# Token lists scattered to DRAM during attention, and expert outputs added into the output by DMA, in a gated cross-attention and mixture-of-experts kernel

## The reference

```python
x = x + tanh(g_xattn) * xattn(layernorm(x), ctx, ctx, Wq, Wk, Wv, Wo, ...)   # 16 heads of width 16
xn = layernorm(x)
probs = softmax(xn @ Wg)                       # N x 8
top_w, top_i = top_k(probs, 2)
top_w = top_w / (sum(top_w) + 1e-8)
combine = sum(one_hot(top_i) * top_w)          # N x 8
y = einsum(square(relu(einsum(xn, W1))), W2)   # every expert; W1 is 8 x 256 x 512, W2 8 x 512 x 256
x = x + tanh(g_ffn) * einsum(combine, y)
```

## Time and profile before

| | us |
|---|---|
| median of 3 runs (lowest to highest) | 647.26 (646.38 to 647.65) |
| span of the profiled execution | 644.1 |
| PE busy | 539.6 (84%) |
| DVE busy | 425.8 (66%) |
| ACT busy | 341.1 (53%) |
| POOL busy | 324.7 (50%) |

### The profile page before, as it was taken

One profiled execution on the slowest core, in us unless ns is written; L12 is line 12 of the kernel. 1 busy time (PEld: TensorE's weight loads), 2 busy tenths in 40 slices (PEclk: granted clock), 3 DMA queues, 4 the chain that ended last, 5 costly groups with the idle time before them and its releaser, 6 DMA issues.

```text
span 644.1 us, 12791 instructions
## 1 busy us (share of the span) xinstructions
PE 539.6 (84%) x3948; PEld 505.0 (78%) x3948; DVE 425.8 (66%) x1132; ACT 341.1 (53%) x716; POOL 324.7 (50%) x423
## 2 busy tenths in 40 slices
PE   4689999999999999996016999999999999999500
PEld 3689999889988999985016899999999999999500
DVE  3657778887888888786997455544445445444287
ACT  3477867676777767662500455555555555555200
POOL 4756745574566546332931555555555555553200
PEclk9899999999999999997555899999999999999955
DMA  7010212112111211112700234333332222221299
GB/s 234 17 34 26 84 50 83 50 52 81 51 66 51 83 50 34 35 41 96 227 0 8 77 119 133 108 108 112 111 107 74 75 82 76 74 77 56 74 390 360
DMA packets 42335, 59.04 MB, mean 92 GB/s; under 512 B 5291, under 2 KB 31583, under 8 KB 42271
## 3 DMA queue, kind: packets, MB, share of 16 engines
q1 hardware_dynamic: 34448, 39.01, 18.1%
q0 software_dynamic: 6944, 18.62, 9.3%
q10 hardware_dynamic: 879, 0.58, 0.3%
HBM read 36.31 MB, written 21.89 MB: 90 GB/s over the span
## 4 chain that ended last, share of the span: by engine, by line
PE 67%; DVE 15%; issue 7%; POOL 4%; DMA 2%; ACT 2%; SPq 1%; DVEq 0%; POOLq 0%; ACTq 0%
PE pair L738 38%; PE pair L837 12%; PE pair L885 4%; DVE x_all L1274 4%; PE pair L921 4%; POOL y_scratch L585 3%; PE pair L929 2%; DVE chosen L982 2%; DVE onehot_row L1154 2%; PE pair L811 2%; PE pair L896 2%; POOL xg L575 2%; PE pair L906 1%; PE pair L803 1%; PE pair L845 1%
## 5 line engine op out<-in xcount | busy, mean ns | idle before, releaser
L585 POOL DMA_INDIRECT y_scratch<-y_sb,scatter_at x71 | 70.0, 986 | 95.5 <-ACT y_sb L701 92.8
L1247 DVE TENSOR_TENSOR hTlo<-pair,hThi 128x512 fp32r<-128x512 f32 x71 | 49.1, 691 | 78.1 <-ACT hThi L715 78.1
L575 POOL DMA_INDIRECT xg<-xn_scratch,gather_at x71 | 69.0, 972 | 44.6 <-DVE gather_at L1208 23.3
L837 PE MATMUL pair<-vals,probT 128*128 128x136 f32 x640 | 87.9, 284 | 2.0 <-ACT probT L609 1.8
L837 PEld LDWEIGHTS pair<-vals,probT 128*128 128x128 f32 x640 | 78.5, 190 | 3.3 <-ACT probT L609 3.1
L738 PE MATMUL pair<-w2hi,hThi 128*128 x284 | 80.6, 284 | 0.1
L738 PE MATMUL pair<-w2hi,hTlo 128*128 x284 | 79.9, 281 | 0.0
L738 PE MATMUL pair<-w2lo,hThi 128*128 x284 | 79.8, 281 | 0.0
L1261 DVE TENSOR_TENSOR hsq<-pair,hrelu 128x512 f32<-128x512 f32 x71 | 49.1, 691 | 44.4 <-ACT hrelu L728 44.3
L728 ACT ACTIVATE hrelu<-pair 128x512 f32<-128x512 f32 x71 | 42.6, 600 | 55.3 <-PE pair L738 55.3
L738 PE MATMUL pair<-w1hi,xgThi 128*128 x142 | 62.5, 440 | 0.0
(11 more groups left out here) (162 smaller groups left out, 1496.1 us busy)
## 6 DMA issues: line engine op xcount, KB each, us to landing
raw<-in_L_ffn_W SPq DMA_DIRECT2D x16, 512.0 KB, 4.2
xs<-in_x SPq DMA_DIRECT2D x16, 256.0 KB, 2.8
x_scratch<-xs SPq DMA_DIRECT2D x32, 128.0 KB, 1.7
xn_scratch<-xn SPq DMA_DIRECT2D x32, 128.0 KB, 1.8
x_all<-x_scratch SPq DMA_DIRECT2D x8, 512.0 KB, 3.9
w1hi<-y_scratch SPq DMA_DIRECT2D x4, 1024.0 KB, 8.9
w1lo<-y_scratch SPq DMA_DIRECT2D x4, 1024.0 KB, 14.4
out<-x_all SPq DMA_DIRECT2D x8, 512.0 KB, 8.7
```

The costliest lines, as they stand in the source:

```text
L575: pool.indirect_dma_start(xg[j % XG][:, :], None, xn2_dram[:, :], bass.IndirectOffsetOnAxis(ap=gather_at[:, j:j + 1], axis=0)).then_inc(d_ ...
L585: pool.indirect_dma_start(y_dram[:, :], bass.IndirectOffsetOnAxis(ap=scatter_at[:, j:j + 1], axis=0), y_sb[j % 2][:, :], None).then_inc(d_ ...
L837: mm = pe.matmul(v_bank[:, 0:UH * VW], probT[u % 2][:, i, :], vals[:, b, c, i, :], start=(i == 0), stop=(i == KC - 1))
L1247: dve.tensor_tensor(hTlo[j % 2][:, :, :].rearrange("p c n -> p (c n)"), bank[2 + j % 2][:, :], hThi[j % 2][:, :, :].rearrange("p c n -> p ...
```

## The change

**Routing on DVE** is done for seven groups of four tiles and two of two (`GROUPS`), with the steps of `route_steps`. `count` starts at N times the expert number, so that `placed` and `at` give at once the place of a choice in a list tensor in DRAM (`list_at`, an integer). The weights are now computed there as well (`part` to `weight1`, one exponential on ACT per group), for each tile and choice into `meta` beside the token number. PE counts with eight products for a group of four (four for one of two).

**The lists** are written by POOL during attention: for each tile and choice one indirect DMA scatters 128 pairs (token number, weight) of 8 bytes into `list_dram`, 64 DMAs in all, four in each of two neighbouring slots per group (`list_stores`). SP fills the list tensor at the start with 3 DMAs (token numbers 0 to 127, weight 0), and for the first block of each expert, by 16 PE products with a one-hot and one more DMA, a token that the expert does not get (`cand_step`). After attention DVE computes from the counts which block of the list is tile j's (`block_at`), POOL gathers 80 blocks of 1 KB by one indirect DMA into `lists`, PE transposes token numbers and weights, DVE copies `gather_at` and ACT copies `tile_w`.

**`w2lo`** is computed by DVE: four of its eight pieces before the copy of `gather_at`, four behind it. All eight pieces of W2 have a buffer of their own.

**The output**: x1 is stored straight to `out` during attention. In the expert stage ACT scales y with `tile_w` as it copies it, and POOL scatters it with `compute_op=ALU.add` into `out`, at the same `gather_at`. As two tiles can hold the same token, the scatter of tile j waits until that of tile j - 1 has landed (`d_acc`). The reload of x1, the loads of `y_dram`, the last additions and the stores of the output are gone; SP waits for the last scatter.

```diff
+        def list_stores(s):

+            for r, (t0, n) in enumerate(GROUPS):
+                first = 2 * (t0 + n - 1) + (14 if r else 17)
+                if first <= s < first + 2:
+                    h = n // 2
+                    return r, [t0 + (s - first) * h + i for i in range(h)]
 ...
+        route_steps = [["best0", "equal0", "lowest0", "key0", "pick0"],
+                       ["masked", "best1", "equal1", "lowest1", "part"],
+                       ["key1", "pick1", "both"],
+                       [None, None, "place", "count", "placed", "at"],
+                       ["sum", "tiny", "one", "inverse", "weight0", "weight1"]]
 @block.sync
...
-                    sp.dma_start(x1_rows[:, t, :], xs[t // GT % XBUF][:, t % GT, :]).then_inc(d_x1[t // GT % XBUF], 16)
+                    sp.dma_start(out_rows[:, t, :], xs[t // GT % XBUF][:, t % GT, :]).then_inc(d_x1[t // GT % XBUF], 16)
...
-            for i in range(2):
-                sp.wait_ge(d_ys[i], 16 * len(range(i, NJ, 2)))
-            for c in range(NT // CT):
-                sp.dma_start(y_in[c], y_rows[:, c * CT:(c + 1) * CT, :, :]).then_inc(d_yin[c], 16)
-            for c in range(NT // CT):
-                sp.wait_ge(v_out, c + 1)
-                sp.dma_start(out_rows[:, c * CT:(c + 1) * CT, :], x1_all[:, c * CT:(c + 1) * CT, :]).then_inc(d_out, 16)
+            sp.wait_ge(d_acc, 16 * NJ)
 @block.gpsimd
...
+                stores = list_stores(s)
+                if stores:
+                    r, tiles = stores
+                    pool.wait_ge(d_cand, 16)
+                    pool.wait_ge(v_meta, 1)
+                    pool.wait_ge(v_route, max(routed_at["at", r], routed_at["weight1", r]))
+                    for t in tiles:
+                        for k in range(CHOICES):
+                            pool.indirect_dma_start(
+                                list_dram[:, :], bass.IndirectOffsetOnAxis(ap=list_at[:, k, t:t + 1], axis=0),
+                                meta[:, t, k, :], None).then_inc(d_list, 16)
...
-            for k in range(E):
-                pool.wait_ge(a_w2hi, k + 1)
-                pool.tensor_tensor(part_of(w2lo, k), raw2[k % W2BUF][:, :], part_of(w2hi, k).bitcast(F32),
-                                   ALU.subtract).then_inc(p_w2lo, 1)
+            pool.wait_ge(d_list, 16 * CHOICES * NT)
+            pool.wait_ge(v_block, 1)
+            pool.indirect_dma_start(lists[0:NJB, :, :].rearrange("p k w -> p (k w)"), None, list_blocks[:, :],
+                                    bass.IndirectOffsetOnAxis(ap=block_at[0:NJB, 0:1], axis=0)).then_inc(d_block, 16)
...
                 pool.wait_ge(a_y, j + 1)
-                pool.wait_ge(v_lists, 1)
-                pool.indirect_dma_start(y_dram[:, :], bass.IndirectOffsetOnAxis(ap=scatter_at[:, j:j + 1], axis=0),
-                                        y_sb[j % 2][:, :], None).then_inc(d_ys[j % 2], 16)
+                if j:
+                    pool.wait_ge(d_acc, 16 * j)
+                pool.indirect_dma_start(out_flat, bass.IndirectOffsetOnAxis(ap=gather_at[:, j:j + 1], axis=0),
+                                        y_sb[j % 2][:, :], None, compute_op=ALU.add).then_inc(d_acc, 16)
 @block.scalar
...
                 if j >= 2:
-                    act.wait_ge(d_ys[j % 2], 16 * (j // 2))
-                act.activation(y_sb[j % 2][:, :], bank[6 + j % 2][:, 0:D], ACT.Copy).then_inc(a_y, 1)
+                    act.wait_ge(d_acc, 16 * (j - 1))
+                act.activation(y_sb[j % 2][:, :], bank[6 + j % 2][:, 0:D], ACT.Copy,
+                               scale=tile_w[:, j:j + 1]).then_inc(a_y, 1)
 @block.tensor
...
+                    dst = shared_place["count", r][:, 0:(n + 1) * E].rearrange("p (t e) -> p t e", e=E)
+                    pe.matmul(dst[:, 0:n, :], counters[:, 0, :], both[:, 0:n, :], start=True, stop=(n == 1))
+                    for i in range(n - 1):
+                        pe.matmul(dst[:, i + 1:n, :], counters[:, 1, :],
+                                  both[:, i:i + 1, :].broadcast_to([P, n - 1 - i, E]), start=False, stop=(i == n - 2))
+                    for i in range(n):
+                        mm = pe.matmul(dst[:, n, :], counters[:, 1, :], both[:, i, :], start=(i == 0), stop=(i == n - 1))
```

More of the change, by code:

```diff
@@ L250, in build @@
-        YW = CT * CHOICES * D
-        y_in = [w[:, i * YW:(i + 1) * YW].bitcast(F32).rearrange("p (t k d) -> p t k d", k=CHOICES, d=D)
-                for w in (w1hi, w1lo) for i in range(E * EW // YW)]
+        need_i = [place(ctx, f"need_i{i}", [P, E], I32) for i in range(2)]
+        need = place(ctx, "need", [P, E])
+        spare = place(ctx, "spare", [P, E])
+        sums = place(ctx, "sums", [P, E, E])
+        taken = place(ctx, "taken", [P, E])
+        ended = place(ctx, "ended", [P, E])
@@ new lines, in route_step @@
+                if kind == "at":
+                    with nc.allow_low_precision(reason="sums of one place below 2 ** 16 and of zeros"):
+                        return dve.tensor_reduce(list_at[:, :, ts], placed[:, :, 0:n, :], AX.X, ALU.add)
+                if kind == "part":
+                    return dve.tensor_tensor(share[:, 0:n, :], logits[:, ts, :], over_e(best[:, 0:n], E + 1), ALU.subtract)
+                if kind == "sum":
+                    dve.wait_ge(a_share, g + 1)
+                    return dve.tensor_reduce(total[:, 0:n], share[:, 0:n, 0:E], AX.X, ALU.add)
@@ new lines, in _ @@
+            link(dve.tensor_reduce(taken[:, :], sums[:, :, :], AX.X, ALU.add))
+            tt(ended[:, :], taken[:, :], C("level"), ALU.is_ge)
+            tt(skipped[:, :], ended[:, :], spare[:, :], ALU.mult)
+            link(dve.tensor_reduce(skip[:, :], skipped[:, :], AX.X, ALU.add))
+            dve.tensor_tensor(block_at[:, :], skip[:, :], C("tile"), ALU.add).then_inc(v_block, 1)
+            link(dve.tensor_reduce(expert[:, :], ended[:, :], AX.X, ALU.add))
+            dve.tensor_scalar(expert[:, :], expert[:, :], float(E - 1), float(EW), ALU.min, ALU.mult).then_inc(v_expert, 1)
@@ new lines, in _, with split_w2 @@
+            dve.wait_ge(t_expert, 1)
+            dve.tensor_copy(expert_at[:, :], bank[7][0:1, 0:P]).then_inc(v_places, 1)
+            def split_w2(k):
+                dve.wait_ge(a_w2hi, k + 1)
+                dve.tensor_tensor(part_of(w2lo, k), raw2[k][:, :], part_of(w2hi, k).bitcast(F32),
+                                  ALU.subtract).then_inc(v_w2lo, 1)
+            for k in range(E // 2):
+                split_w2(k)
+            dve.wait_ge(t_lists, 1)
+            dve.tensor_copy(gather_at[:, :], bank[6][:, 0:NJB]).then_inc(v_gather, 1)
@@ L1244, in _ @@
+            for k in range(E // 2, E):
+                split_w2(k)
             for j in range(-3, NJ):
```

447 lines of the change are left out of this document (191 added, 256 removed).

## The result

The changed kernel takes 725.92 us (median of 4 runs, 724.88 to 730.69); the kernel before took 647.19 us on the same chip. The ratio is 1.123, with a 95% interval of 1.1193 to 1.1267: slower by 79 us, where 627 us was forecast. The time lies above the forecast's range too (593 to 677).

A forecast was written before the change was run, and what follows sets the result against it. PE was taken to bound attention and the expert stage, a DVE chain the gap, memory traffic with DVE the end. 644.1 + 12 - 24.4 + 27.2 - 34.4 = 624.5 us of span, forecast 627 us, range 593 to 677.

The forecast's parts named there:

- The expert stage, forecast +27.2: Expert stage: serial adding scatters slow the pace from 3.49 to 3.8 us over 70 steps, adding 27.2 us.
- Rival 2: Expert stage: DRAM read and write come one after the other; slower overall from a 4.08 us pace, 677 us; chance 0.25.
- the ring: Expert stage loop: one scatter's start to landing, 3.5 us, plus 0.3 us until the next DMA starts; pace 3.8 us.
- The round trip: Expert stage: an adding scatter's start to landing, taken as 3.5 us; up to 3.2 us was held free.
- Attention, forecast +12: Attention: list scatters on POOL delay `xnTlo` and PE gets 48 more products; together taken as 12 us more.
- Upper bound +35: Attention: each list scatter takes 1.5 us, later norm scales stall ACT, and all of it reaches PE: 35 us more.
- rival 3: Attention: list scatters cost 35 us instead of 12, with the forecast's pace: 650 us; chance 0.08.
- Between the stages, forecast -24.4: Gap before the expert stage: after 16 list scatters and the gather, PE starts at 331.1 instead of 355.55, saving 24.4 us.
- The end, forecast -34.4: After the last scatter: loads, additions and stores go; 3.5 us of landing and 0.1 for SP remain, saving 34.4 us.

The follow-up runs named there:

- lists_spread: The changed kernel with one list scatter per attention slot instead of four in each of two slots, last two groups unchanged: 719.5 us, ratio 1.1094 to the kernel before.
- no_add: The changed kernel with a plain scatter in place of the adding one, all waits kept, output rows overwritten: 642.5 us, ratio 0.9937 to the kernel before.
- two_targets: The changed kernel with odd tiles added into a scratch tensor, each target with its own chain of waits, merge left out: 636.5 us, ratio 0.9843.
- no_cand: The changed kernel without the step that finds tokens outside each expert for the first blocks: 722.3 us, ratio 1.1136 to the kernel before.
- w1lo_slot1: The changed kernel with the w1 pieces one slot earlier in attention: 719.1 us, ratio 1.1087 to the kernel before.
- w2lo_last: The changed kernel with all eight `w2lo` pieces behind the copy of `gather_at`: 732.9 us, ratio 1.1306 to the kernel before.
- best1: dist2 with list scatters spread over the slots, no step for tokens outside each expert, and w1 pieces one slot earlier: 606.4 us, ratio 0.9367 to the kernel before.
- lists_late: The changed kernel with all 64 list scatters behind POOL's attention work: 769.1 us, ratio 1.1893 to the kernel before.
- dist2: The changed kernel with each adding scatter waiting for the last but one, and list padding naming tokens from the middle: 637.5 us, ratio 0.9834 to the kernel before.

## Why the prediction was wrong

**The expert stage, forecast +27.2, measured +87.1.** This step failed first. The mechanism was right: one DMA in flight, a wait in each tile, everything else at the scatters' pace. Rival 2 stated it and named its point: slower from a pace of 4.08 us. Two terms of the ring were too small. The round trip was taken as 3.5 us and is 3.81 on the mean: 70 x 0.31 = 22 us. The time from a landing to the next start was taken as 0.3 us and is 0.79: 70 x 0.49 = 34 us. The six long steps add 4. Together 60, the whole miss of 59.9. The second is the graver: it also lowers the round trip that is free, from 3.2 us to 3.49 - 0.79 = 2.7. The 0.3 us came from two DMA instructions that POOL had queued and could start one behind the other. That POOL slept before is not the difference. In the kernel before it had waited 23.30 us for DVE's `gather_at`, and its DMA instruction at 351.30 started 0.29 us behind the end of

```profile
350.81 0.20 DVE L1208 TENSOR_SCALAR gather_at<-code 128x71 int32<-128x71 f32 x1
```

In `lists_spread` it started 0.27 us behind the landing of a DMA of SP (125.62 + 14.8 = 140.42, then 140.69). The 0.77 to 0.79 us stand where POOL waited for the landing of an indirect DMA that it had issued itself. No row of the kernel before has that case, and why it takes longer is open. This term is also why the range failed: its upper end, 4.2 + 0.3 = 4.5 us a step, varied the round trip and kept the gap fixed. `no_add` and `two_targets` fix the blame: without the add 82 of the 87 us are gone (243.8 against 238.8 us from first to last scatter), without its being serial all of them (238.7).

By the rule cited of the Trainium skill (Collectives: The Full Stack), the add costs a second read and an estimated 0.3 us; the trace has 3.8 us against 2.4, so 1.4 us. It doesn't bear this rule out as a price for latency, though as one for throughput nothing here speaks against it (`two_targets`).

**Attention, forecast +12, measured +40.6.** The bunches of list scatters do delay `xnTlo`, as the prediction said, but by more: PE waited 3.0 to 3.2 us in three groups, and 4.33 in the one with `klo`, where 1.6 was worked out. The prediction took the phase of the kernel before and moved the queue in it; its forecast put nothing on the norm scale, 1.7 us late in its own working, which only the upper bound names. The norm scale holds ACT, that holds the exponential and the transpositions, and PE comes to the next wait late and slow (granted clock 0.94 against 0.99). Upper bound +35 was meant for this and was too low, since two further costs were missing. DVE's `outside` and `onehot` work was not counted at all, only its 16 PE products: 7 us by `no_cand`. And `placed` beside `w1lo`: the earlier trace rows has that very operation at 2.37 us beside POOL's `w2lo`, and the prediction noted it where it went, without asking where else it would stand beside a wide POOL operation: in most routing groups (the median of its nine instances is 2.04 us). Moving it off gave 7 us (`w1lo_slot1`). With the 23 us of the list scatters that makes 37 of the 39 us by which attention fell behind. The 81 us that rival 3 added to POOL count all 64 list scatters; 16 of them stand behind attention.

**Between the stages, forecast -24.4, measured -16.6.** The order was right: a row of list scatters on POOL, then the lists' gather. Missing: 4.4 us of the scatter of 5.32 us; 1.3 us, as the last scatter landed 3.66 us after its start, not 2.4; 0.8 us from that landing to POOL's next DMA, again; and 1.2 us for the first rows, which reach PE 5.8 us after the gather's start instead of 4.25, of which the working had 0.3 to spare. That is 7.7 of 7.8 us. The rule on DVE and POOL's descriptors, which the prediction cited from the Trainium skill (SBUF — State Buffer, section "SBUF: two separate sides") and put aside for a row of 1.13 us, is stated there for operations in a two-port mode. Its part "Who interferes with whom" says that a `tensor_tensor`, which `w2lo` is, has no two-port mode and contends with GpSimd's reads only, and it infers that such an operation does not stall descriptor writing. The trace differs: a list scatter took 5.32 us over four operations of 4.61 together, and none was long once they were moved (`w2lo_last`). The row it was weighed against had DVE operations of 0.2 to 0.7 us beside it; that these let POOL in between is likely and not shown.

**The end, forecast -34.4, measured -32.1.** Right but for size: 5.9 us remain instead of 3.6. No instruction follows the last scatter, and it lands after 3.8 us, 0.3 more than forecast; the other 2.1 us lie between that landing and the end of the span, where 0.1 was put down. What fills them, the trace does not show.

The sum of the misses is 59.9 + 28.6 + 7.8 + 2.3 = 98.6 us, the distance from 624.5 to 723.1.

## What to carry to other kernels

When a change puts one DMA at a time into a loop, price the ring as the landing plus the time until the next start, take that time from a row in which the engine waited for a landing of its own queue, or call it unknown, and look at how few microseconds of slack it has; then ask whether the order is needed at distance one, since a distance of two took back the whole 87 us here. A queue engine that shares its time with short DMAs wants them spread over its slots: 48 scatters of 1.26 us cost some 23 us in bunches, and in `best1`, where they are spread, all of attention falls behind by 4.9 us. Where wide operations of VectorE and GpSimd met here, one was held by the other, so lay out both engines' wide work in one table before moving any.

## What the runs showed of the hardware

- An indirect scatter with add (128 rows of 1 KB) occupies GpSimd's queue for 1.58 us, and a plain one for 0.98 us; it lands 3.8 us after its start, against 2.4. With rows of half the size it is still 1.58, and about 3.4.
- From the landing of an indirect DMA of GpSimd's own to the start of the DMA instruction that waited for it there: 0.77 to 0.79 us. It is 0.30 us between two that are queued, 0.29 us behind the end of a VectorE instruction that it waited for, and 0.27 us behind the landing of a DMA of SyncE (one row).
- An 8-byte list scatter that starts beside four back-to-back `w2lo` (VectorE, tensor_tensor of 128x1024 from SBUF, 4.61 us together) takes 5.32 us instead of 0.96; a gather of 1 KB rows beside such operations takes 1.71 to 1.97 us instead of 0.95. A tensor_tensor of VectorE (`placed`) takes 2.22 us beside a tensor_tensor of GpSimd of 2.37 us, and has a median of 0.37 us where that is moved.
- The last list scatter, 8 bytes for each of 128 partitions, landed 3.66 us after its start in the changed kernel, 4.68 in best1, 5.54 in w2lo_last, 3.46 in lists_late and 2.42 in dist2. In the changed kernel, lists_late and dist2 the loads of W2 were over by then (DMA share 0.01 to 0.02), so neither these loads nor the small size alone explains the spread; the cause is open.
- Two adding scatters into the same tensor, the second started before the first had landed, ran at 3.41 us a tile in `dist2`, with PE as the bound.
